# Linear attention and routed convolution on one core: value weights applied to a k-weighted sum of inputs, k's maximum folded elementwise, routing product without rstd

## What is computed

```
x = x + attention(groupnorm(x))          # 32 groups of 4 channels
x = x + condconv(groupnorm(x))

attention(x):                            # 4 heads of 32 channels, N = 1024 pixels
  xn  = rmsnorm(x) * g1                  # over channels, per pixel
  q, k, v = w_qkv @ xn                   # 3 x 128 channels
  k, v = [mem_k, k], [mem_v, v]          # 4 learned columns in front
  q = softmax(q over a head's channels) * 32**-0.5
  k = softmax(k over the 1028 positions)
  context = k @ v.T                      # per head, 32 x 32
  out = w_out @ (context.T @ q) + b_out
  return rmsnorm(out) * g2

condconv(x):
  pooled = 4 x 4 means of x
  y = relu(rconv_w @ pooled + rconv_b)   # 16 x 16 = 256 values
  r = sigmoid(relu(fc_w @ y + fc_b))     # 3 experts x 128 input channels
  w = sum_k r[k] * expert_weight[k]      # a 3 x 3 filter for each image
  return conv3x3(x, w)
```

## Time and profile before

| | us |
|---|---|
| median of 3 runs | 489.87 (489.65 to 490.08) |
| profiled execution, its own time | 490.54 |
| span of the profiled execution | 488.7 |
| TensorE busy | 434.4 (89% of the span) |
| VectorE busy | 384.1 (79%) |
| ScalarE busy | 276.9 (57%) |
| GpSimd busy | 244.0 (50%) |

### The profile page before, as it was taken

One profiled execution on the slowest core, in us unless ns is written; L12 is line 12 of the kernel. 1 busy time (PEld: TensorE's weight loads), 2 busy tenths in 40 slices (PEclk: granted clock), 3 DMA queues, 4 the chain that ended last, 5 costly groups with the idle time before them and its releaser, 6 DMA issues.

```text
span 488.7 us, 8419 instructions
## 1 busy us (share of the span) xinstructions
PE 434.4 (89%) x2398; PEld 370.8 (76%) x2398; DVE 384.1 (79%) x754; ACT 276.9 (57%) x828; POOL 244.0 (50%) x244
## 2 busy tenths in 40 slices
PE   2649676899999999999999999999999999998786
PEld 1438565788888878888788888888888888877575
DVE  3461488989798979899898979898989888896631
ACT  2354648384857565766748484757575757643110
POOL 4403436565727365554556573827366665433240
PEclk9986969799999999999999999999999999999899
DMA  7202024241607070524334250707070513233511
GB/s 217 118 0 86 3 86 174 85 175 56 246 1 302 1 274 28 196 105 150 151 119 182 77 223 14 286 0 300 1 270 32 189 70 146 114 114 145 213 46 43
DMA packets 18779, 61.53 MB, mean 126 GB/s; under 512 B 2992, under 2 KB 4032, under 8 KB 18752
## 3 DMA queue, kind: packets, MB, share of 16 engines
q1 hardware_dynamic: 18752, 61.21, 33.2%
HBM read 19.29 MB, written 8.39 MB: 57 GB/s over the span
## 4 chain that ended last, share of the span: by engine, by line
PE 57%; issue 15%; DVE 13%; POOL 8%; ACT 5%; POOLq 1%; DMA 1%; DVEq 0%; ACTq 0%
PE ps_conv L1150 26%; PE ps_att L1088 7%; PE ps_qkv L1068 3%; PE ps_qkv L1070 3%; PE ps_qkv L1069 3%; POOL rstd L445 3%; PE ps_qkv L1104 3%; DVE k_diag L764 2%; PE ps_stat L1127 2%; DVE q_max L779 2%; ACT qkv L570 2%; PE ps_qkv L1055 2%; POOL route_prod L498 2%; POOL pooled_n L491 2%; PE ps_att L1086 1%
## 5 line engine op out<-in xcount | busy, mean ns | idle before, releaser
L570 ACT ACTIVATE qkv<-ps_qkv,scale 128x384 f32<-128x384 f32 x128 | 70.4, 583 | 27.6 <-PE ps_qkv L1070 24.6
L476 POOL TENSOR_TENSOR q_exp<-q_exp,q_rsum 128x1024 f32<-128x1024 f32 x16 | 30.6, 1914 | 88.3 <-DVE q_rsum L800 88.3
L508 POOL TENSOR_TENSOR w_lo<-w_full,w_hi 128x1152 fp32r<-128x1152 f32 x16 | 42.5, 2659 | 55.9 <-ACT w_hi L629 39.5
L582 ACT ACTIVATE q_exp<-q_exp 128x1024 f32<-128x1024 f32 x16 | 17.0, 1061 | 68.1 <-DVE q_exp L786 68.1
L1068 PE MATMUL ps_qkv<-wqkv_hi,x_hi 128*128 128x384 f32 x128 | 45.6, 356 | 5.3 <-ACT qkv L570 4.7
L594 ACT ACTIVATE q_t<-ps_qkv 128x512 f32<-128x512 f32 x32 | 19.1, 597 | 49.0 <-PE ps_qkv L1104 49.0
L1069 PE MATMUL ps_qkv<-wqkv_lo,x_hi 128*128 128x384 f32 x128 | 43.9, 343 | 0.0
L1070 PE MATMUL ps_qkv<-wqkv_hi,x_lo 128*128 128x384 f32 x128 | 43.9, 343 | 0.0
L1150 PE MATMUL ps_conv<-left_hi,w_lo 128*128 128x512 f32 (+1 forms) x96 | 41.3, 431 | 0.0
L1150 PE MATMUL ps_conv<-img_hi,w_hi 128*128 128x512 f32 x96 | 38.0, 396 | 3.7 <-POOL w_lo L508 3.7
L466 POOL TENSOR_TENSOR x_lo<-x,x_hi 128x1024 fp32r<-128x1024 f32 x16 | 38.0, 2375 | 6.3 <-ACT x_hi L559 6.3
(11 more groups left out here) (137 smaller groups left out, 1263.5 us busy)
## 6 DMA issues: line engine op xcount, KB each, us to landing
xa<-in_x_dram SPq DMA_DIRECT2D x16, 512.0 KB, 3.8
xb<-in_x_dram SPq DMA_DIRECT2D x16, 512.0 KB, 4.7
out_dram<-expert_raw SPq DMA_DIRECT2D x16, 512.0 KB, 2.9
left_hi<-img_hi SPq DMA_DIRECT2D x16, 511.5 KB, 2.9
right_hi<-img_hi SPq DMA_DIRECT2D x16, 511.5 KB, 3.7
left_lo<-img_lo SPq DMA_DIRECT2D x16, 511.5 KB, 4.3
right_lo<-img_lo SPq DMA_DIRECT2D x16, 511.5 KB, 4.9
expert_raw<-_conv_expert_weight_dram SPq DMA_DIRECT2D x1, 1728.0 KB, 9.2
```

The costliest lines, as they stand in the source:

```text
L476: nc.gpsimd.tensor_tensor(q_exp[:, :, :], q_exp[:, :, :], q_rsum[:, :].unsqueeze(2).to_broadcast((128, NT * HEADS, DH)), ALU.mult).then_in ...
L508: nc.gpsimd.tensor_tensor(w_lo[p][:, :, :].rearrange("p t o -> p (t o)"), w_full[:, :], w_hi[p][:, :, :].bitcast(F32).rearrange("p t o -> ...
L570: nc.scalar.activation(qkv[:, t, 0:QKV], ps_qkv[t % 2][:, 0:QKV], ACT.Copy, scale=scale1[:, t:t + 1]).then_inc(qkv_done, 1)
```

## The change

The columns of w_qkv that make v are no longer projected. project multiplies by 256 columns instead of 384. The normalised input itself takes v's place: x_copy (ScalarE) copies the transposed image out of ps_qkv into x_nt after each half of squares1, and x_scale (GpSimd) multiplies x_nt by scale1. key_contexts sums k_exp times x_nt over the pixels (with the columns of ones, and mem_ones for the learned columns). The result is evacuated (k_x), transposed, evacuated again (x_k), and contexts multiplies it by the value weights wqkv_t and adds the learned columns' part. The head mask is applied by context_mask; the division by the softmax sum moves to mix_evacuate. context_transpose is gone.

k_partial_max was one reduction over a strided view; it is now three elementwise maxima (8 tiles to 4, to 2, to 1). k_diagonal, a 128 x 128 product, becomes k_maximum_all on one column, and k_shift multiplies a broadcast of that column by the identity in float32. memk_diag is gone from the set-up.

route_prod is made from pooled_c, without rstd; routing multiplies by a broadcast of rstd instead of ones. In GpSimd's step the routing product stands ahead of rstd. In TensorE's step the group variances, mixes and both transposes of the next image keep together and routing stands later, with single convolution products between. w_first lives in a part of expert_raw that is free by then.

```diff
@@ gpsimd @@
+            def x_scale(b, p):
+                pool.wait_ge(x_nt_done, 2 * (b + 1))
+                pool.wait_ge(scale1_done, b + 1)
+                nc.gpsimd.tensor_tensor(x_nt[:, :, 0:C], x_nt[:, :, 0:C],
+                                        scale1[:, :].unsqueeze(2).to_broadcast((128, NT, C)),
+                                        ALU.mult).then_inc(x_scaled_done, 1)
...
-                                        pooled_n[:, :].unsqueeze(1).to_broadcast((128, RC, SP * SP)),
+                                        pooled_c[:, :].unsqueeze(1).to_broadcast((128, RC, SP * SP)),
@@ scalar @@
+            def x_copy(b, p, h):
+                if past(b, 1):
+                    act.wait_ge(k_x_ps, b)
+                act.wait_ge(ssq1_sum_done, 2 * b + h + 1)
+                nc.scalar.activation(x_nt[:, NT // 2 * h:NT // 2 * (h + 1), 0:C],
+                                     ps_qkv[h][:, :].rearrange("p (t c) -> p t c", c=C), ACT.Copy).then_inc(x_nt_done, 1)
...
-                nc.scalar.activation(qkv[:, t, 0:QKV], ps_qkv[t % 2][:, 0:QKV], ACT.Copy, scale=scale1[:, t:t + 1]).then_inc(qkv_done, 1)
+                nc.scalar.activation(qk[:, t, :], ps_qkv[t % 2][:, 0:QK], ACT.Copy, scale=scale1[:, t:t + 1]).then_inc(qkv_done, 1)
...
+                nc.scalar.activation(k_x[:, :], ps_att[:, 0:C], ACT.Copy).then_inc(k_x_done, 1)
...
+                nc.scalar.activation(x_k[:, :], ps_att[:, 0:HID], ACT.Copy).then_inc(x_k_done, 1)
@@ vector @@
-                v.tensor_scalar(memk_diag[:, :], ident[:, :], memk_max[:, :], None, ALU.mult).then_inc(setup_dve, 1)
...
+                v.tensor_tensor(k_half[:, :, :], k[:, 0:NT // 2, :], k[:, NT // 2:NT, :], ALU.max).then_inc(k_half_done, 1)
...
+                v.tensor_tensor(k_quarter[:, :, :], k_half[:, 0:NT // 4, :], k_half[:, NT // 4:NT // 2, :], ALU.max).then_inc(k_quarter_done, 1)
...
-                v.tensor_reduce(k_max_part[:, :], qkv[:, :, HID:2 * HID].rearrange("p t c -> p c t"), AX.X, ALU.max).then_inc(k_part_done, 1)
+                v.tensor_tensor(k_max_part[:, :], k_quarter[:, 0, :], k_quarter[:, 1, :], ALU.max).then_inc(k_part_done, 1)
...
-                v.scalar_tensor_tensor(k_diag[:, :], ident[:, :], k_max[:, :], memk_diag[:, :], ALU.mult, ALU.max).then_inc(k_diag_done, 1)
+                v.tensor_tensor(k_max_all[:, :], k_max[:, :], memk_max[:, :], ALU.max).then_inc(k_max_all_done, 1)
@@ tensor @@
-                    pe.wait_ge(ssq1_sum_done, 2 * b + t + 1)
+                    pe.wait_ge(x_nt_done, 2 * b + t + 1)
...
-                mm(ps_att[:, 0:HID], ones_r[:, :], k_diag[:, :], start=True, stop=True).then_inc(k_shift_ps, 1)
+                mm(ps_att[:, 0:HID], k_max_all[:, :].to_broadcast((128, 128)), ident[:, :], start=True, stop=True).then_inc(k_shift_ps, 1)
...
+                mm(ps_att[:, 0:HID], memv_t[:, :], memk_exp[:, :], start=True, stop=False)
+                mm(ps_att[:, 0:HID], wqkv_t[:, QK:QKV], x_k[:, :], start=False, stop=True).then_inc(context_ps, 1)
```

198 lines of the change are left out of this document (114 added, 84 removed).

## The result

| | us |
|---|---|
| before, median of 4 runs beside it | 489.98 (489.65 to 490.56) |
| after, median of 4 runs | 519.98 (515.33 to 522.84) |
| ratio | 1.060 (1.052 to 1.068) |
| profiled execution of after, its own time | 522.84 |
| its span | 521.1 (before 488.7) |

The account below looks back on a forecast made before the run. Each step was taken as Y + R, with R one rigid chain and Y lengthened by x_scale in GpSimd's queue. Span 488.7 - 2.5 + 28.9 - 1.0 = 514.1, plus 1.84 around it 515.9, given as 515; range 491 to 522.

Parts of the forecast that it names:

- the forecast case: Slower by GpSimd's queue, x_scale delaying scale2 and so y_scaled: 509 to 522 us, chance 0.63.
- The step: One of thirteen repeated steps, Y + R: from 26.08 us to 28.3, +29 over the thirteen.
- Y: From TensorE's contexts to VectorE's next y_scaled: from 12.86 us to 14.9, with 0.2 more for the hold.
- The hold: x_scale on GpSimd holding up VectorE's short two-operand routing instructions, delaying scale2 by up to 0.4 to 0.5 us; taken as 0.2.
- The rival in which x_scale does not delay y_scaled: VectorE's own list places y_scaled: Y 13.5, step 26.7, 495 us; within the one-half-wrong case, chance 0.15.
- y_scaled waits for scale2: Sign in the changed trace: y_scaled comes 14.5 to 15.4 us behind contexts, and scale2 is what it waits for.
- The predicted idle us of VectorE ahead of y_scaled: Sign in the changed trace: VectorE idles about 1 us a step ahead of y_scaled, where there was next to none.
- R: From y_scaled to TensorE's next contexts, one rigid chain: stays 13.22 us, as k_maximum_all still waits for w_lo's end.
- Fill: The steps before the full pattern: memk_diag's 2.24 us goes, gains and losses sum to -2.5 us, ends -6 and 0.
- Drain: Two last steps that still route: pooled_n's 0.52 us goes from the path, -1.0 us, ends -2.5 and 0.
- TensorE's 0.75 us of saved list: TensorE's own work falls by 0.75 us a step, but this is hidden as a longer wait at k_shift.
- the removed routing wait: The removed wait of routing gives nothing in the steps: hidden, it turns into a longer wait at k_shift.

Follow-up runs that it names:

- e2: The kernel before plus one GpSimd pass of x_scale's shape, result unused, between scale1 and scale2 (w_first moved to make room): 511.93 us, ratio 1.044.
- e1: The changed kernel with x_scale moved in GpSimd's list from between scale1 and scale2 to behind w_lo: 503.27 us, ratio 1.029.
- e4: The kernel before without the projection of v, 256 instead of 384 columns, v left at a constant 1: 484.62 us, ratio 0.989.
- e5: e1 with k's maximum kept in PSUM, so that k_max_all reads one operand from SBUF: 502.73 us, ratio 1.027.
- e10: The kernel before with the routing part of the change alone: 479.90 us, ratio 0.980.
- e6: e1 without the two copies x_copy on ScalarE, so part of the computation is left out: 491.39 us, ratio 1.003.
- e8: e1 with the copies on VectorE, k's maximum in PSUM and k's softmax put ahead of q's: 559.83 us, ratio 1.138.
- e9: e8 without its swap, so q_subtract is again ahead of k_subtract: 490.14 us, ratio 1.002.

## Why the prediction was right, and where its terms were off

The forecast was 515 for a median of 519.98, inside its range of 491 to 522. Sign and mechanism held, and the forecast case is the one that came. The closeness is in part luck: the profiled execution took 522.84, where the forecast's terms add up to 515.9. The steps came out 1.5 us shorter than forecast, fill and drain 4.6 and 4.0 longer.

**The step, predicted 28.3, measured 28.20.** +27.4 us over thirteen steps for a predicted +29. **Y, predicted 15.1, measured 15.26.** The squares start 271.45 - 264.80 = 6.65 behind contexts for a forecast of 6.4; the first sum of squares at 9.55 for 9.3; scale1 1.65, x_scale 1.90, scale2 1.64 for 1.64, 1.91 and 1.64. *The hold* was placed at the routing's short instructions and put at 0.2. In after it fell on the second sum of squares itself, which has one data operand, and cost 1.0 of VectorE's time. But scale2 stands behind x_scale anyway, so it starts only 0.1 us later than GpSimd is free. Where it does fall on the routing's instructions, in e2, it holds one for 1.7 us and delays scale2 by 0.6 more than GpSimd's queue would (by the estimate there). *The rival in which x_scale does not delay y_scaled* falls by e1, and e2 shows the delay in the kernel before. *y_scaled waits for scale2* is half right: gate_n ended at 280.12 and scale2 at 280.03, a tie, since the held sum of squares pushed the routing back as well. The predicted idle us of VectorE ahead of y_scaled was therefore not there; it stood at the first sum of squares (1.73 us, had 0.61 at its place).

**R, predicted 13.22, measured 12.91.** k_max_all waits for the end of w_lo, at 1.33 us instead of the forecast 0.7 or more: as argued. The 0.3 lie ahead of it. w_full starts 3.21 us behind y_scaled against 3.46 before, since residual2 between them no longer waits 0.20 us for TensorE, and w_lo starts 6.04 behind y_scaled against 6.30. The same 0.3 is in e4 (the shorter projections) and in e2 (a later y_scaled, with all 384 columns), so either is enough for it. R was not as rigid as the earlier trace rows made it look: in the kernel before it is 13.02 to 13.27 over the steps.

**Fill, predicted -2.5, measured +2.05.** This term has the wrong sign. Its sum leaves out what the sentence before it names: the first delay of scale2 in the third step, 2.0 us by the forecast's own Y. With it the term would have been -0.5. The k_shifts of the three images show where the rest went: 32.13, 62.65 and 88.78 before, 29.68, 61.56 and 90.83 after. The first comes 2.45 earlier (memk_diag and the first fold stood ahead of it), then the second step loses 1.36 and the third 3.14. From contexts to the next transposes the third step took 7.97 us against 6.24, 1.7 in one step where 0.9 stood, and from the transposes to the second pair of projections 6.68 against 5.89. The place of x_scale is 0.9 of the fill (after to e1). But e5, with the same work in the fill as e1 but for one operand, needed 1.0 less, and e10, whose edit was to change nothing there, 2.0 less than before. So what share the longer chain has stays open.

**Drain, predicted -1.0, measured +3.0.** The last convolution took 15.3 us instead of 12.5, 2.8 of the 3.0. The 14 us shown above have a granted clock of 0.82. The 14 us of before at the same distance from its end:

```profile
470.70:484.70 14.00, 12.53 (x55) 10.06 (x54) 1.38 (x2) 0.00 (x0) 1.58 (x1) 1.00 0.09 37
```

e1, with the same tail but for x_scale, had 1.00 there and a drain of 59.3. By the traces the clock stood at 0.50 for 10.2 us of after's drain (which makes the 0.92 shown above), 3.4 of before's, 0.7 of e1's and 11.0 of e5's. If half of that time is taken off (an estimate of what the clock cost, as TensorE was busy in most of it), after's drain is 58.6, before's 59.0, e1's 58.9 and e5's 58.7. By this estimate the clock accounts for the drain's difference, and what the change itself did there is about -0.4. What lowers it is not settled: TensorE idled 2.81 us ahead of the last convolution in after, where the clock fell, and 2.82 in e1, where it did not. The spread of after's runs, 7.5 us, stays open as well: their mean granted clocks, 0.957 to 0.966, do not follow their times.

**What was hidden and what was not.** The forecast called TensorE's 0.75 us of saved list and the removed routing wait hidden. In after they are: TensorE waits 10.2 us at k_shift and 21.4 for evacuations, and VectorE idles 0.77 us for the squares ahead of the second sum. In the kernel before they are not: alone they give 0.29 (e4) and 0.58 a step (e10). What went wrong is the reading of the earlier trace rows: scale2 waited 0.99 us for "VectorE's sum of squares", and I took the squares to be what made that late. It was the queue ahead of it, the routing, which waited for TensorE, which waited for GpSimd. The 0.5 us by which the mean step exceeds TensorE's work was mostly this, 0.43 by the wait list. The total did not suffer, since Y of after was built up from its contexts at 0, with no wait of before in it.

**The account of the 2.11 us a step.** By the runs: x_scale's place 1.01 (after to e1), the copies on ScalarE 0.84 (e1 to e6), and 26.33 is left against 26.07. That rest is R, 0.31 shorter, and Y, 0.57 longer. The traces split Y: from contexts to the first square it is 5.76 us before, 6.62 in after and 6.61 in e6 (means of the twelve steps). So the longer chain ahead of the transposes costs 0.85, for a forecast of 0.9 there, and from the first square to y_scaled e6 is 0.28 faster than before. That the routing gives these 0.28 is likely and was not tested: on the kernel before it gave 0.55 of Y.

## What to carry to other kernels

Read each engine's own queue for what a new pass stands in front of, and what short instructions of another engine run beside it. Here the change saved TensorE a third of a projection (worth 5 us on the kernel before), and its product of 1.9 us on GpSimd was put between two short steps on which everything else waits; moving that product alone gained 17 us. Work is cheap only on an engine and at a place that the chain does not pass. And test the parts of a bundle singly: this change as a whole was 6% slower, while two of its small parts (a routing product taken out from behind a slow rstd, and one column in place of a diagonal matrix, here with the maximum kept in PSUM) make the kernel 3.2% faster than before.

## What the runs showed of the hardware that was not expected

- A scaling of 8 elements a partition with one data operand (tensor_scalar in float32) was held for 1.04 us beyond its 0.172 by GpSimd's two-operand pass, to within 0.02 us of the pass's end. The forecast had looked for holds only on instructions with two operands. The same section of the Trainium skill, "Who interferes with whom", lists tensor_scalar among the operations that can take the shared port pair in their two-port modes; no run here tells which mode this one was in.
- The hold does not scale with the instruction: one element a partition waited 1.3 us for w_lo's end, and 256 elements 1.7 us for the end of e2's pass. With its operand in PSUM the one-element instruction took 0.158 beside the same w_lo.
- Moving two instructions of the softmax cost 70 us (e8 against e9). About 3.0 of the 4.9 us a step are the granted clock, by the estimate above: it stood at 0.50 for six us of the step shown, after three nearly idle ones.
